# Attention's hardware loop over heads: four heads a pass, then eight

## The reference

```python
ada = silu(c) @ W_ada + b_ada                       # shift, scale, gate, twice
h = modulate(layernorm(x), shift_msa, scale_msa)
q, k, v = split(h @ W_qkv + b_qkv)                  # 16 heads of 36
scores = einsum('blhd,bmhd->bhlm', q * D**-0.5, k)
attn = softmax(scores, axis=-1)
o = einsum('bhlm,bmhd->blhd', attn, v)
x = x + gate_msa * (o @ W_proj + b_proj)
h = modulate(layernorm(x), shift_mlp, scale_mlp)
x = x + gate_mlp * (gelu(h @ W_fc1 + b_fc1) @ W_fc2 + b_fc2)
x = x + ((x @ U) @ R - x @ U) @ U.T                 # U = qr(P), R = expm(A(cond))
```

## Time and profile before

| | |
|---|---|
| median of 3 runs | 3248.59 us (3247.25 to 3250.45) |
| the profiled execution | 3243.69 us |
| its span, first to last instruction | 3242.0 us |
| attention's PE work, first `scores` to last | 742.5 to 1859.4 us of the span |
| backward branches at L682, per engine | 15 executed, 14 of them taken |

### The profile page before, as it was taken

The page is one execution under the profiler, slowest core; times in us unless marked ns, Lnnn a source line. Parts: engine busy times, 40 slices in busy tenths (PEclk is TensorE's granted clock), DMA queues, the critical chain, the costliest instruction groups (busy, mean ns, idle before and its releaser), DMA issues. The chain is left out here.

```text
span 3242.0 us, 49779 instructions
## 1 busy us (share of the span) xinstructions
PE 2883.0 (89%) x16066; PEld 2287.0 (71%) x16066; DVE 1637.1 (50%) x2847; ACT 1460.9 (45%) x1863; POOL 1432.2 (44%) x1065
## 2 busy tenths in 40 slices
PE   6759899979999999999999868759999999999976
PEld 2247777855566666666666557659999999999965
DVE  3446556547888888888888645511111111111125
ACT  2112222227888888898888825531111111111112
POOL 1232322216888888888888824422222222222210
PEclk9769999988999999999999978879999999999988
DMA  5365556553433433334334157785111111211153
GB/s 178 129 224 206 194 199 220 179 188 74 90 79 87 90 78 89 88 80 89 82 84 91 48 164 246 209 263 164 46 60 35 62 44 35 70 36 35 50 152 136
DMA packets 340330, 378.72 MB, mean 117 GB/s; under 512 B 167008, under 2 KB 230120, under 8 KB 340188
## 3 DMA queue, kind: packets, MB, share of 16 engines
q1 hardware_dynamic: 328494, 354.69, 36.7%
q0 software_dynamic: 4224, 9.44, 1.6%
q10 hardware_dynamic: 7474, 12.68, 1.3%
HBM read 226.82 MB, written 158.93 MB: 119 GB/s over the span
## 5 line engine op out<-in xcount | busy, mean ns | idle before, releaser
L770 POOL TENSOR_TENSOR a_pl<-a_pf,a_ph 128x1024 fp32r<-128x1024 f32 x384 | 913.4, 2399 | 46.8 <-ACT a_pf L858 46.0
L793 DVE TENSOR_REDUCE a_mx<-a_psum_s 128x1 f32<-128x1024 f32 x496 | 606.2, 1222 | 177.1 <-PE a_psum_s L869 169.0
L856 ACT ACTIVATE a_ph<-a_psum_t 128x1024 fp32r<-128x1024 f32 x512 | 526.2, 1028 | 143.9 <-PE a_psum_t L901 125.2
L1504 PE MATMUL m_psum_h<-m_ht,m_w 128*128 128x256 f32 x4032 | 532.6, 283 | 31.5 <-DMA m_w<-w_s 22.5
L1456 POOL TENSOR_TENSOR m_al<-m_af,m_ah 128x256 fp32r<-128x256 f32 x288 | 212.2, 737 | 763.7 <-DVE m_ah L1465 763.7
L1504 PEld LDWEIGHTS m_psum_h<-m_ht,m_w 128*128 128x128 f32 x4032 | 507.3, 189 | 35.3 <-issue 35.3
L1465 DVE CAST m_ah<-m_af 128x256 fp32r<-128x256 f32 x288 | 84.6, 294 | 848.5 <-ACT m_af L1442 848.5
L1518 PE MATMUL m_psum_y<-m_w,m_ah 128*128 128x288 f32 x2304 | 505.4, 296 | 1.4 <-DVE m_y L1482 1.4
L1442 ACT ACTIVATE m_af<-m_psum_h,m_bias 128x256 f32<-128x256 f32 x288 | 137.0, 476 | 814.2 <-PE m_psum_h L1504 814.2
L920 PE MATMUL a_psum_o<-a_ph,a_vs 128*100 128x512 f32 x1024 | 405.8, 396 | 3.8 <-POOL a_pl L770 3.7
L921 PE MATMUL a_psum_o<-a_pl,a_vs 128*100 128x512 f32 x1024 | 404.6, 395 | 0.0
(11 more groups left out here) (222 smaller groups left out, 3108.8 us busy)
## 6 DMA issues: line engine op xcount, KB each, us to landing
a_qs<-q_s SPq DMA_DIRECT2D x192, 144.0 KB
a_ks<-k_s SPq DMA_DIRECT2D x192, 144.0 KB
w_s<-q_ws SPq DMA_DIRECT2D x64, 324.0 KB, 3.4
h_s<-p_ht SPq DMA_DIRECT2D x40, 512.0 KB, 5.2
m_ht<-h_s SPq DMA_DIRECT2D x16, 1280.0 KB, 7.8
v_s<-q_vo SPq DMA_DIRECT2D x64, 288.0 KB, 2.3
a_vs<-v_s SPq DMA_DIRECT2D x128, 144.0 KB, 4.6
q_s<-q_qko SPq DMA_DIRECT2D x32, 512.0 KB, 2.7
```

The lines of the kernel that those rows point to most:

```text
L770: pool.tensor_tensor(pl[:, s % RING], pf[:, s % RING], raw(ph[:, s % RING]), ALU.subtract).then_inc(lo_pool, 1)
L793: dve.tensor_reduce(mx[:, u % 2, t:t + 1], p_s[:], AX.X, ALU.max).then_inc(s_free, 1)
L856: act.activation(ph[:, s % RING], p_t[:, s % 2], ACT.Exp, scale=SCALE)
L1504: m = pe.matmul(p_h[:, f % RING, 0:GM], w1[:, k, f * P:(f + 1) * P], ht[:, q, a], start=(i == 0), stop=(i == len(PASSES) - 1))
```

## The change

The loop's body is written out for eight heads instead of four. `turn` runs over 0 and 1, so every slot occurs twice in a pass. n is NHEAD // SLOTS = 16, so the loop makes 7 passes (56 heads) where it made 15 (60 heads), and the last two groups of four, eight heads, stand behind it; only the last of them has `last` set. The order of each engine's work within and across heads is unchanged.

```diff
--- before.py
+++ after.py
@@ -678,12 +678,15 @@
 
         def heads(eng, body):
 
+
             n = NHEAD // SLOTS
-            with eng.Fori(0, n - 1) as i:
+            with eng.Fori(0, n // 2 - 1) as pair:
+                for turn in range(2):
+                    for u in range(SLOTS):
+                        body(2 * SLOTS * pair + SLOTS * turn + u, u, 2 * pair + turn, False)
+            for i in (n - 2, n - 1):
                 for u in range(SLOTS):
-                    body(SLOTS * i + u, u, i, False)
-            for u in range(SLOTS):
-                body(SLOTS * (n - 1) + u, u, n - 1, True)
+                    body(SLOTS * i + u, u, i, i == n - 1)
 
         def lo_counts(n_heads, s):
```

## The result

The changed kernel takes 3262.3 us (median of 10 runs, 3258.36 to 3272.24); beside them the kernel before took 3247.92 us (10 runs). The ratio is 1.0052 with a 95% interval from 1.0039 to 1.0066: slower by 0.5%. The forecast was 3260.8 us. The profiled span grew from 3242.0 to 3261.3 us. Attention, from the first `scores` to the last, grew from 742.5 to 1859.4 us (1116.9) to 743.2 to 1876.7 us (1133.5), by 16.6 of the 19.3 us.

What follows compares the result with a forecast made beforehand. Attention was taken as paced by PE and the engines it meets. Table loads saved (-3.4 us) and six SP stalls (+15.6 us) gave +12.2 us on 3248.59: 3260.8 us, range 3249 to 3267.

Steps and rivals of the forecast that it cites:

- 8 passes' starts of 0.43 us: In attention, eight fewer loop passes each save 0.43 us, ended by ACT's table load: 3.4 us gained.
- One reading: In attention, DVE and PEld wait for each other in every step, some tenths of a microsecond each.
- the count of blocks: Program is held in blocks of 128 instructions: three are held across a loop's branch, four are not.
- the third limit: Block limit 302 instructions into SP's body; the new body of 326 passes it by 24, so lies in four blocks.
- The price of a stall: At each of SP's six taken branches PE stands 2.6 us (1.5 to 3.1): 15.6 us in all.
- the slack: Lateness SP's small DMAs can have before PE's scores wait: between nothing and 1.4 us, taken as 0.4.
- The 3.43 us from DVE: DVE's idle time at its qkv loop's branch, used for the upper end of SP's added stall, 3.1 us.
- "No refetch": Rival: SP's body of 326 instructions is held, only the table loads count: 3245.2 us; chance 0.12.
- the buffer of 512 instructions: The Trainium skill's figure for engines but PE; by it alone SP's 326 would stay, the sum being -3.4 us.
- The window of two pages: The Trainium skill's rule that a branch target outside it waits for a fetch; by it SP's new body misses.
- "Mostly covered": Rival: SP's stall happens but PE catches up, 0.75 us each come through: +1.1 us, 3249.7 us; chance 0.06.
- "A second engine": Rival: ACT or DVE refetches as well, some 3.1 us more per branch: 3279.4 us; chance 0.05.

Runs made afterwards that it cites:

- the run with SP at four: The changed kernel, but SP keeps four heads a pass while PE, DVE, ACT and POOL take eight: attention 1114.0 us, ratio 0.9977 to the kernel before.
- the one with ACT written out: The kernel before, with ACT's 64 heads written out without a loop, the other engines at four a pass: attention 1111.2 us, ratio 0.998.
- The padding: Semaphore increments on SP ahead of its loop in the changed kernel: attention 1114.1 us with 56 of them, 1136.4 us with 38.
- the run with 56 increments: The changed kernel with 56 semaphore increments on SP ahead of its loop: attention 1114.1 us, ratio 0.9979 to the kernel before.
- the run with sixteen heads: The kernel before, but ACT takes sixteen heads a pass, a body of 515 instructions: attention 1114.5 us, whole time 3247.15 us (one run).
- the loop cut at another place: The changed kernel, SP's order of work unchanged, but its loop's branch stands behind the four small DMAs: attention 1115.6 us, ratio 0.9981 to the kernel before.
- the run with 20 increments: The kernel before with 20 semaphore increments at the start of each SP pass of four heads: attention 1131.8 us (one run).
- the run with 40: The kernel before with 40 semaphore increments at the start of each SP pass of four heads: attention 1150.6 us (one run).
- SP alone at eight: The kernel before, but SP alone takes eight heads a pass, the others four: attention 1135.0 us, ratio 1.0052.
- the 38 increments: The changed kernel with 38 semaphore increments on SP ahead of its loop: attention 1136.4 us (one run).

## Why the prediction was right

*The gain.* 8 passes' starts of 0.43 us were right, and ACT was the engine behind them: the run with SP at four lost 2.9 us of attention, the one with ACT written out 5.7 us for 14, both 0.4 us each. The four heads moved out of the loop were put at nothing; the written-out heads take up to 0.07 us more each, 0.3 us in all. One reading was too broad: the earlier trace rows show 4 and 6 waits in 18 us, about a head of eight steps, and not one in every step. Nothing in the sum hangs on it.

*That SP refetches, and only SP.* Right at each of the six taken branches, and by the count of blocks: the third limit passed by 24 instructions, ACT, DVE and POOL within what is held, PE as well. The packets at 920.4, 974.0 and 1028.6 us show the three limits, and the last of them shows that a block is still fetched in the pass's last head, 10 us ahead of the branch that then waits. The padding moved the stall away and back where the reckoning put the limit. Queue 14 got 36 packets more where I had 25 to 30. The step that carried this was to look for both kinds of branches in the trace before, and the earlier trace rows, and then to place SP's limit by one fetch.

*The price of a stall.* I had 3.0 - 0.4 = 2.6 us. SP was later by 2.56 us on average (branch to next instruction 2.58 to 3.18 us, less 0.3), the slack 0.2 to 0.4 us, PE's wait 13.1 / 6 = 2.2 us, and with its edges 2.34 us per head: 14.0 us instead of 15.6. The 3.43 us from DVE were over what any of SP's gaps took.

*What was missing.* The fall of the clock: 5 x 1.28 = 6.4 us in the profiled execution. The sum of what was seen is -3.4 + 14.0 + 6.4 = 17.0 us, and attention's 16.6 us agree with it, its first head being 0.9 us shorter and its last ones a little longer. So the mechanism was right and one term was missing: against the 17.0 us the forecast of 12.2 us is 4.8 us short, a clock left out (6.4 us) less a stall taken 1.6 us too dear in all. That the medians, 14.4 us apart, lie nearer to the forecast is in part luck: executions of the changed kernel differ by more (3258.36 to 3272.24 us) than the miss.

*The rivals.* "No refetch" fell, and with it the buffer of 512 instructions read as a plain capacity ("Runtime: NRT & Kernel Launch" of the Trainium skill, section "Instruction fetch mechanics"): SP's body of 326 instructions is refetched at one place and held at another, 10 instructions behind a limit. The window of two pages, by which the prediction let SP's body miss, was taken from that section of the Trainium skill without working it out. With the 128 instructions of queue 14's packets it would hold 256, and the run with 56 increments held 326 in three blocks; with the 256 that the Trainium skill gives, only every second of the limits at 46, 174 and 302 would count, and the body would miss with 46 and 302 and stay with 174. The trace has a packet of 8 KB at all three. "Mostly covered" fell: PE gave back nothing of the stall. "A second engine" did not happen, and its price was wrong: I had 3.1 us for a refetch on ACT, the run with sixteen heads showed 1.3 us. What I said of SP's loads, that they are not late, was true for this change and not with much to spare, as the loop cut at another place showed.

## What to carry to other kernels

Before a loop's body is made longer, count instructions per engine and look in the trace for branches followed by 3 us of nothing, and for packets on the instruction queue during steady passes. Treat the queue engine like any other: SP was idle for a third of each head, yet 0.2 to 0.4 us of lateness at one place was all it could afford. Where a refetch can't be avoided, cut the loop where that engine waits anyway; and a table load that a compiler puts at the head of a loop's body is paid at every pass, so written-out heads on that one engine took 5.7 us off attention, where the change without its stall took 2.9 us.

## What the runs showed of the hardware that I had not expected

Short idle times of PE cost twice. In a stretch where PE otherwise worked with gaps of at most 0.83 us at a granted 1.00, the 14 waits of the run with 20 increments (0.91 to 1.29 us) were followed by no fall of the clock. Of the 14 of the run with 40 (1.97 to 2.02 us) four were, and of the 18 of the changed kernel, of SP alone at eight and of the 38 increments (1.90 to 2.56 us) fifteen. The length alone doesn't decide: in the changed kernel the wait of 2.36 us had no fall behind it and that of 1.90 us had one. What does decide, no run here shows. Each of these falls lowered the clock to the 1.2 GHz level for 3.4 us and cost 1.3 to 1.5 us on top of the wait. In the run with 40 increments, where nothing is refetched, the time behind one stall looks as it did after the change (table by windows):

```profile
1058.00:1061.40 3.40, 3.40 (x11) 2.50 (x10) 1.23 (x1) 2.74 (x3) 1.68 (x2) 0.61 0.79 220
```

And the program is held in blocks. On SP a backward branch went on at once when the body touched at most three blocks of 128 instructions, and waited when it touched four. The packet at the third limit fits this: it is fetched at 1028.6 us, when SP enters its fourth block, and the branch at 1038.9 us then waits. Five packets a pass for four touched blocks mean that one is fetched ahead, so room for four blocks, the one ahead included, would fit every SP body seen. That the fifth takes the place of the first is argued, for no row shows what a packet overwrites. For DVE and ACT only bodies far over three blocks (428 to 515 instructions) were seen to be refetched, so that their limit is the same is argued too, not shown.
